# Making one matrix product's operand in halves of the samples, in a four-stage residual kernel

## The reference

```python
x = x + conv1d(x, w0, taps=9, groups=4) + (cond @ cw.T + fside)[:, :, None]
for l in (1, 2, 3):
    att = softmax(mlp_l(cond))                       # 8 weights for each sample
    x = x + einsum('bk,koi->boi', att, w_l) @ x + (att @ bias_l)[:, :, None]
```

## Time and profile before

| | |
|---|---|
| median of 3 runs | 327.9 us (327.82 to 328.38) |
| the profiled execution | 329.1 us, its span 327.3 us |
| TensorE matmuls busy | 317.1 us, 97% of the span |
| VectorE busy | 253.0 us, 77% |
| ACT busy | 227.6 us, 70% |
| GpSimd busy | 158.8 us, 49% |
| granted TensorE clock | 1.00 throughout |
| DMA | 104.80 MB, mean 320 GB/s |

### The profile page before, as it was taken

One profiled execution on the slowest core, in us unless ns is written; L12 is line 12 of the kernel. 1 busy time (PEld: TensorE's weight loads), 2 busy tenths in 40 slices (PEclk: granted clock), 3 DMA queues, 4 the chain that ended last, 5 costly groups with the idle time before them and its releaser, 6 DMA issues.

```text
span 327.3 us, 5950 instructions
## 1 busy us (share of the span) xinstructions
PE 317.1 (97%) x1479; PEld 256.4 (78%) x1479; DVE 253.0 (77%) x231; ACT 227.6 (70%) x344; POOL 158.8 (49%) x269
## 2 busy tenths in 40 slices
PE   8899999999999999999999999999999999999993
PEld 8787868888888787688788887777888887888862
DVE  4593968788886886977888867788788878887674
ACT  5445597777777778776767777787777676777662
POOL 8001289887444454545544445555555454444500
PEclk9999999999999999999999999999999999999999
DMA  7994356998999999989998999998999999897658
GB/s 255 262 289 172 132 208 222 356 375 354 349 332 348 362 334 364 345 322 359 371 355 335 339 338 354 336 373 340 341 365 366 346 357 365 320 353 291 267 212 340
DMA packets 29948, 104.80 MB, mean 320 GB/s; under 512 B 3353, under 2 KB 3609, under 8 KB 21978
## 3 DMA queue, kind: packets, MB, share of 16 engines
q1 hardware_dynamic: 29940, 104.70, 86.2%
HBM read 36.53 MB, written 33.55 MB: 214 GB/s over the span
## 4 chain that ended last, share of the span: by engine, by line
PE 76%; DMA 8%; issue 6%; DVE 6%; ACT 2%; POOL 1%; DVEq 0%; POOLq 0%
PE bank L394 43%; PE bank L430 8%; DMA ybuf<-conv_sb 8%; PE bank L432 7%; PE bank L431 7%; PE bank L402 4%; PE bank L509 2%; DVE mix_lo L739 1%; ACT conv_sb L594 1%; PE bank L438 1%; PE bank L451 1%; POOL a_dup L359 1%; DVE ybuf L729 1%; DVE x_lo L715 1%; ACT x_hi L587 1%
## 5 line engine op out<-in xcount | busy, mean ns | idle before, releaser
L349 POOL COPY a_diag<-table 64x64 f32 (+1 forms) x128 | 87.7, 685 | 117.6 <-PE bank L402 85.1
L594 ACT ACTIVATE conv_sb<-bank 128x512 f32<-128x512 f32 x128 | 76.6, 598 | 70.6 <-PE bank L394 66.3
L715 DVE TENSOR_TENSOR x_lo<-x_sb,x_hi 128x2064 fp32r<-128x2064 f32 x32 | 74.0, 2312 | 41.6 <-ACT x_hi L587 40.4
L394 PE MATMUL bank<-x_hi,toep_hi 128*128 128x512 f32 x256 | 84.5, 412 | 0.0
L394 PE MATMUL bank<-x_lo,toep_hi 128*128 128x512 f32 x256 | 80.7, 397 | 0.0
L394 PE MATMUL bank<-x_hi,toep_lo 128*128 128x512 f32 x256 | 80.5, 396 | 0.0
L359 POOL COPY a_dup<-table 64x128 f32 (+1 forms) x128 | 64.4, 503 | 30.8 <-DVE table L803 13.2
L729 DVE TENSOR_TENSOR ybuf<-ybuf 128x2048 fp32r<-128x2048 f32 x31 | 72.1, 2324 | 1.7 <-ACT ybuf L598 1.6
L614 ACT ACTIVATE out_sb<-bank,beta 128x512 f32<-128x512 f32 x93 | 63.7, 687 | 4.6 <-PE bank L432 1.6
L587 ACT ACTIVATE x_hi<-x_sb 128x2064 fp32r<-128x2064 f32 x32 | 61.6, 1924 | 3.1 <-DMA x_sb<-in_x 2.9
L394 PEld LDWEIGHTS bank<-x_hi,toep_lo 128*128 128x128 f32 x256 | 48.3, 189 | 12.0
(11 more groups left out here) (83 smaller groups left out, 172.9 us busy)
## 6 DMA issues: line engine op xcount, KB each, us to landing
x_sb<-in_x SPq DMA_DIRECT2D x32, 1032.0 KB, 7.5
ybuf<-conv_sb SPq DMA_DIRECT2D x128, 256.0 KB, 4.5
out<-out_sb SPq DMA_DIRECT2D x30, 1024.0 KB, 7.7
out_sb<-conv_sb SPq DMA_DIRECT2D x4, 256.0 KB
out<-out_sb SPq DMA_DIRECT2D x4, 256.0 KB, 3.0
out<-x_sb SPq DMA_DIRECT2D x4, 256.0 KB, 3.3
early<-in_pairs SPq DMA_DIRECT2D x1, 640.0 KB, 4.6
x_sb<-in_toep SPq DMA_DIRECT2D x1, 640.0 KB, 6.1
```

The costliest lines, as they stand in the source:

```text
L349: nc.gpsimd.tensor_copy(a3_diag[rows, par, :, C * h + NH * e:C * h + NH * e + NH], table[0][C * e:C * e + C, here, h, :]).then_inc(comp_in, 1)
L394: last = mm(o, w[:, d, g, :], v[:, par, g, :, d:d + J], start=i + d == 0, stop=i + d == 3)
L594: nc.scalar.activation(conv_sb[:, par, g, :], conv_ps[g % banks][:, :], ACT.Copy).then_inc(conv_out, 1)
L715: nc.vector.tensor_tensor(x_lo[:, par].rearrange("p g s j -> p (g s j)"), x_sb[:, par].rearrange("p g s j -> p (g s j)"), x_hi[:, par].rea ...
```

## The change

VectorE makes y_hi and y_lo of a step in two operations each, one for samples 0 and 1 (h = 0) and one for samples 2 and 3 (h = 1), each 128x1024 instead of 128x2048 elements. In a loop step the order becomes: x_lo, y_hi half 0, the output add, y_lo half 0, the mix_lo pair, y_hi half 1, y_lo half 1. The semaphores yhi_set and ylo_set count two for each step. TensorE's first mix waits for the first halves, and the mix of sample 2 for the second halves. SyncE's first move waits for both halves of y_lo of two steps before. For the step NQ - 2 both halves are made ahead of mix_lo, and y_lo of step 0 is two operations in a row; the last step keeps its halves.

```diff
 move(q, par, g):
                 if g == 0:
-                    wait(sp, ylo_set, q - 1)
+                    wait(sp, ylo_set, 2 * q - 2)
 mix(q, par, s):
                 if s == 0:
-                    pe.wait_ge(*((yhi_first, 1) if ... q == NQ - 1 else (yhi_set, q + 1)))
-                    pe.wait_ge(ylo_set, q + 1)
+                    pe.wait_ge(*((yhi_first, 1) if ... q == NQ - 1 else (yhi_set, 2 * q + 1)))
+                    pe.wait_ge(ylo_set, 2 * q + 1)
                     pe.wait_ge(mixlo_set, 2 * q + 2)
-                if isinstance(q, int) and q == NQ - 1 and s == S // 2:
-                    pe.wait_ge(yhi_set, NQ)
-                    pe.wait_ge(ylo_set, NQ + 1)
+                if s == S // 2:
+                    pe.wait_ge(yhi_set, 2 * q + (1 if ... q == NQ - 1 else 2))
+                    pe.wait_ge(ylo_set, 2 * q + 2)
 VectorE:
+            def y_half(t, par, h):
+                return t[:, par, :, S // 2 * h:S // 2 * h + S // 2, :]
+
+            def y_high(q, it, par, h):
+                if h == 0:
+                    dve.wait_ge(moved[par], 16 * G * it + 16 * G)
+                    wait(dve, mix_done, 4 * q - 4)
+                nc.vector.tensor_copy(y_half(y_hi, par, h), y_half(y_sb, par, h)).then_inc(yhi_set, 1)
+
+            def y_low(q, par, h):
+                dve.wait_ge(yhi_set, 2 * q + h + 1)
+                nc.vector.tensor_tensor(y_half(y_lo, par, h), y_half(y_sb, par, h),
+                                        y_half(y_hi, par, h).bitcast(F32), ALU.subtract).then_inc(ylo_set, 1)
...
-            y_low(0, 0)
+            y_low(0, 0, 0)
+            y_low(0, 0, 1)
             mix_low(0, 0)
...
-                y_high(q - 1, it_prev, 1 - par)
+                y_high(q - 1, it_prev, 1 - par, 0)
                 finish(q - 2, it - 1, par, 1)
-                y_low(q - 1, 1 - par)
+                y_low(q - 1, 1 - par, 0)
                 mix_low(q - 1, 1 - par)
+                y_high(q - 1, it_prev, 1 - par, 1)
+                y_low(q - 1, 1 - par, 1)
...
-            y_high(NQ - 2, NQ // 2 - 1, 0)
-            y_low(NQ - 2, 0)
+            for h in range(2):
+                y_high(NQ - 2, NQ // 2 - 1, 0, h)
+                y_low(NQ - 2, 0, h)
             mix_low(NQ - 2, 0)
```

More of the change, by code:

```diff
@@ L409, in mix @@
                 if s == 0:
-                    pe.wait_ge(*((yhi_first, 1) if isinstance(q, int) and q == NQ - 1 else (yhi_set, q + 1)))
-                    pe.wait_ge(ylo_set, q + 1)
+                    pe.wait_ge(*((yhi_first, 1) if isinstance(q, int) and q == NQ - 1 else (yhi_set, 2 * q + 1)))
+                    pe.wait_ge(ylo_set, 2 * q + 1)
                     pe.wait_ge(mixlo_set, 2 * q + 2)
-                if isinstance(q, int) and q == NQ - 1 and s == S // 2:
-                    pe.wait_ge(yhi_set, NQ)
-                    pe.wait_ge(ylo_set, NQ + 1)
+                if s == S // 2:
+                    pe.wait_ge(yhi_set, 2 * q + (1 if isinstance(q, int) and q == NQ - 1 else 2))
+                    pe.wait_ge(ylo_set, 2 * q + 2)
                 if isinstance(q, int) and q == NQ - 2:
@@ L598, in y_high @@
                 nc.scalar.activation(y_hi[:, par].rearrange("p h s j -> p (h s j)"),
-                                     y_sb[:, par].rearrange("p h s j -> p (h s j)"), ACT.Copy).then_inc(yhi_set, 1)
+                                     y_sb[:, par].rearrange("p h s j -> p (h s j)"), ACT.Copy).then_inc(yhi_set, 2)
             def mix_high(q, par):
@@ L852, in _ @@
             step(NQ - 2, NQ // 2 - 1, 0, NQ // 2 - 2)
-            y_high(NQ - 2, NQ // 2 - 1, 0)
-            y_low(NQ - 2, 0)
+            for h in range(2):
+                y_high(NQ - 2, NQ // 2 - 1, 0, h)
+                y_low(NQ - 2, 0, h)
             mix_low(NQ - 2, 0)
             finish(NQ - 3, NQ // 2 - 2, 1, 1)
[L858 to L862, removed]
             mix_low(NQ - 1, 1)
             dve.wait_ge(moved[1], 16 * G * (NQ // 2))
-            nc.vector.tensor_copy(y_hi[:, 1, :, 0:S // 2, :], y_sb[:, 1, :, 0:S // 2, :]).then_inc(yhi_first, 1)
-            y_low_half(0)
-            y_low_half(1)
+            nc.vector.tensor_copy(y_half(y_hi, 1, 0), y_half(y_sb, 1, 0)).then_inc(yhi_first, 1)
+            dve.wait_ge(yhi_first, 1)
+            nc.vector.tensor_tensor(y_half(y_lo, 1, 0), y_half(y_sb, 1, 0), y_half(y_hi, 1, 0).bitcast(F32),
+                                    ALU.subtract).then_inc(ylo_set, 1)
+            dve.wait_ge(yhi_set, 2 * NQ - 1)
+            nc.vector.tensor_tensor(y_half(y_lo, 1, 1), y_half(y_sb, 1, 1), y_half(y_hi, 1, 1).bitcast(F32),
+                                    ALU.subtract).then_inc(ylo_set, 1)
             finish(NQ - 2, NQ // 2 - 1, 0, 1)
```

## The result

The changed kernel takes **325.74 us** (median of 6 runs, 325.4 to 326.91) where the kernel before takes 328.08 (6 runs): a ratio of 0.9927, 95% interval 0.9906 to 0.9947. Two later series of the same kernel gave 325.67 and 325.64, ratios 0.9915 (0.9884 to 0.9946) and 0.9922 (0.9894 to 0.9950). So it is faster by 2.3 to 2.5 us; 325.0 was forecast. The profiled execution took 325.4 us, its span 323.6. A ratio can differ from the quotient of two medians, by up to 0.4% here; its interval says more.

What follows compares the result with a forecast made beforehand. TensorE, busy 250.32 of 252.00 us in the loop, was taken as the bound, with 3.8 us of stall: -3.8 + 0.6 + 0.3 = -2.9, so 326.2 profiled and 325.0 as median; range 324.2 to 327.5.

Steps and rivals of the forecast that it cites:

- 3.8 us of stall are all that the loop can give: TensorE in the loop: 27 steps take 243.04 us, 239.3 at its own pace of 8.86 a step.
- the chain is 1.64 shorter: VectorE in the loop, from y's landing to the end of the mix_lo pair: 3.41 us instead of 5.05.
- 0.6 of the stalls stays: TensorE in the loop: late loads still hold it at three places, 0.2 us each (bounds 0 and 3.8).
- The ends cost 0.3: Prologue and tail: added half operations on the critical path, +0.08 before the first mix and 0.2 in the tail.
- Sum: -2.9, then 1.2 less for runs without a profile: Whole kernel: -3.8 + 0.6 + 0.3 takes the profiled 329.1 us to 326.2; the unprofiled median, 1.2 below, to 325.0.
- The second half behind the mix_lo pair costs nothing: Loop: y_lo complete 1.95 us after the mix_lo pair, without cost to TensorE, the next x_lo or SyncE's first move.
- a held move: Rival, SP's queue: y_lo's second half delays the first move, 0.2 us in each of 27 steps, 330.4 us; chance 0.06.
- the next landing: SP's queue: where a held first move would do harm, by delaying the store, the three moves and y's next landing.
- Transfers didn't give it back: Rival, loop: later loads return half the gain (326.3 us, chance 0.15) or all of it (328.2, chance 0.10).
- GpSimd wasn't shut out: Rival, loop: VectorE's second half blocks GpSimd's copies, a third of a us a step, 334 us; 0.03 with anything unnamed.
- The edit does what it says: Rival denied here: transfer or mix_hi sets TensorE's late waits, so halves don't help; 328.2 us, sharing the chance 0.10.

Runs made afterwards that it cites:

- 5.35: The changed kernel with both halves of y_hi and y_lo made ahead of the mix_lo pair: 331.0 us, ratio 1.0071.
- 3.98: The changed kernel with y_hi one whole cast again in the loop and only y_lo in halves: 325.5 us, ratio 0.9921.
- the kernel with whole ends: The changed kernel with whole operations for y_lo of step 0 and y of step NQ - 2, halves only in the loop: 325.59 us, ratio 0.9919.

## Why the prediction was right, point by point

- *3.8 us of stall are all that the loop can give, and the chain is 1.64 shorter.* Right: the profile lost 3.74 in 27 steps, the chain is 3.45 us, and the experiments on either side of it (5.35; 3.98, and the output add moved ahead) show that what stands between the landing and the mix_lo pair is the cause.
- *0.6 of the stalls stays.* Too much for the profile: none stayed. x_hi still waits for its load (3.2 us in all; 2.9 before), but never long enough to hold TensorE.
- *The ends cost 0.3.* The chains got longer about as worked out, but nothing of it is seen in the medians. In the tail 3.58 became 3.84 and is hidden behind TensorE's second group; in the prologue, where 0.08 was forecast, mix_lo started 2.33 after the start of y_lo instead of 2.21, so 0.12.
- *Sum: -2.9, then 1.2 less for runs without a profile.* The profiled execution gives -3.7 us, 0.8 more than the sum, because none of the stalls stayed and the ends cost nothing that shows. The step to the median failed the other way: the profiled execution of before was 1.0 us above its median (329.1 against 328.08), that of after 0.3 below (325.4 against 325.74), so -3.7 becomes -2.3. Two errors, of 0.8 and 1.5 us, partly cancel, and that the forecast of 325.0 came within 0.7 us of 325.74 is to that extent luck. The mis-sized term behind the second is most likely the first one of the sum: **3.8 us of stall was that of one execution**, perhaps one with more than usual, and taking the difference to the median off by a constant kept such an excess in. No run without a profile has a trace, so what the stall is in the median execution isn't shown.
- *The second half behind the mix_lo pair costs nothing, since SP's first move waits for ACT's copy.* Right, in every step. That a held move would be dear was right too (some 24 us for moves that start 3 to 4 us late in each step); its place, "the next landing" of y, was wrong: it is the load's.
- *The rivals.* Transfers didn't give it back; GpSimd wasn't shut out: no compose waits in the loop. The edit does what it says.

## What to carry to other kernels

When an engine without slack waits a few times at one place, list what runs between the late event and the wait's release, and take out of it whatever that wait doesn't need. Order can do as much as splitting: moving one 0.67 us operation in front of a landing that is waited for anyway gave the gain of all the halves. Check what the displaced work frees, though: here it frees the buffer of the next transfer, and the cover over that was 0.8 us at its thinnest, with some 24 us behind it. Where the same median can be had with a thin margin or a wide one (0.13 us with the output add ahead, 1.04 with halves), only the profile tells them apart.

## What the runs showed of the hardware

**Halves let GpSimd in.** I had feared the contrary. GpSimd's a_diag copies fell from 685 to 416 ns in the mean, while its a_dup copies rose from 503 to 566; together its busy time fell from 158.8 to 132.5 us, although VectorE is busy 11 us more. The order counts as well as the length: in the kernel with whole operations and the output add ahead the a_diag copies take 867 ns and the a_dup copies 391. A copy that starts while y_lo is being made ends only after it, in all 67 cases in the loops of the two kernels; beside the output add, which reads a PSUM bank, 58 of 103 ended before it, and took as little as 0.23 us. Beside a whole y_lo a_diag copies took up to 2.38 us, beside a half up to 1.27 (each the longest of its loop); first before, second after:

```profile
60.15 2.38 POOL L349 COPY a_diag<-table 64x64 f32 x1 [0.19 <-POOL a_dup L359]
```

```profile
59.89 1.27 POOL L349 COPY a_diag<-table 64x64 f32 x1 [0.17 <-POOL a_diag L349]
```

At a place where the copy starts later in the half, it is

```profile
122.89 1.01 POOL L349 COPY a_diag<-table 64x64 f32 x1 [0.16 <-POOL a_diag L349]
```

It ends at 123.90; the half of y_lo beside it (1.26 us from 122.54) ends at 123.80. The Trainium skill (SBUF — State Buffer, the section on the two separate sides) has the rule for it: VectorE, with two inputs in SBUF or in a two-port mode, and GpSimd hold a shared pair of ports for a whole instruction, and the other waits. By that rule the length of one VectorE instruction bounds the wait, and the trace agrees: 2.38 beside the y_lo of 2.28 us, 1.27 beside a half of 1.22.

**One late load in the prologue, paid twice.** In the profile of the kernel with whole ends TensorE waits there for the load of the bias matrices:

```profile
PE bank L485 <- DMA early<-in_mixrow: 2.5, 1, 2.5
```

Soon after this wait, which ends at 20.25, the granted clock is at its lower level (0.50, 1.2 GHz) although TensorE is busy, and then back at 1.00:

```profile
20.00:21.00 1.00, 0.75 (x2) 0.49 (x3) 0.65 (x1) 0.00 (x0) 0.00 (x0) 1.00 1.03 278
22.00:25.00 3.00, 3.00 (x16) 3.00 (x16) 0.49 (x1) 0.60 (x1) 0.00 (x0) 0.50 1.00 340
26.00:30.00 4.00, 4.00 (x22) 3.09 (x20) 1.87 (x4) 1.54 (x4) 0.93 (x4) 1.00 0.18 73
```

The first mix comes at 50.23 us instead of 46.64, 3.6 us late. The wait is 2.5 of them, and three busy us at half the clock can give up to 1.5 more, so the two together are enough for it. The execution took 329.23 us where the kernel's median is 325.59, and the loop behind is as fast as ever but for one step of 9.04. Five other profiles have the same wait with 0.3 to 1.1 us and one with 1.5; the rest, those before and after among them, don't have it. How much of the scatter of runs without a profile comes from it isn't shown. Differences of half a us can't be read from medians of this kernel; they can be from the chain of a profile.
